# Finishing steps of graph blocks spread over more places of a pipeline, and GpSimd's gathers without a wait in mid group

## What is computed

```
x = gatv2(embed, src, dst, Wl1, ..., heads=4)      # pass 2
x = relu(x)
x = gatv2(x, src, dst, Wl2, ..., heads=1)          # pass 3
# gatv2: xl = x @ Wl + bl ; xr = x @ Wr + br
#   score = (leaky_relu(xl[src] + xr[dst], 0.2) * att).sum()
#   alpha = exp(score - max) / sum over the edges of dst
#   out   = segment_sum(xl[src] * alpha, dst) + bias
# typed layer, twice (its edges: passes 4 and 5):
#   k, q, v = typed_linear(x, ntype, Wk / Wq / Wv)    # one of 8 matrices by node type
#   kw, m   = per head and edge type matrices on k[src], v[src]
#   a = (kw * q[dst]).sum(-1) * pri / sqrt(16);  alpha = segment softmax of a
#   out = silu(typed_linear(segment_sum(alpha * m), ntype, Wa))
#   out = layernorm(out * al + x * (1 - al)) * g + b
```

## Time and profile before

| what | value |
|---|---|
| median of 3 runs | 7276.15 us (7275.86 to 7287.23) |
| profiled execution, its own time | 7268.52 us |
| its span, first to last instruction | 7266.8 us |
| busy share of the span: PE, DVE, ACT, POOL | 68%, 69%, 24%, 66% |
| mean granted clock of TensorE | 0.777 of full |
| HBM traffic over the span | 173 GB/s |

### The profile page before, as it was taken

One profiled execution on the slowest core, in us unless ns is written; L12 is line 12 of the kernel. 1 busy time (PEld: TensorE's weight loads), 2 busy tenths in 40 slices (PEclk: granted clock), 3 DMA queues, 4 the chain that ended last, 5 costly groups with the idle time before them and its releaser, 6 DMA issues. The chain is left out here.

```text
span 7266.8 us, 92453 instructions
## 1 busy us (share of the span) xinstructions
PE 4960.7 (68%) x26319; PEld 4144.5 (57%) x26319; DVE 5007.5 (69%) x14623; ACT 1751.7 (24%) x5241; POOL 4810.0 (66%) x5008
## 2 busy tenths in 40 slices
PE   2555555667775777777687877876777776666666
PEld 2444444666664555665466666655666665566665
DVE  4434434777775888888677777766777775788886
ACT  2334332222222222222122222221222222121111
POOL 3777776777775777776555665537666662777774
PEclk8676766777777888777777887777888887787887
DMA  4544445666664444444344444437666664666665
GB/s 132 169 159 160 159 160 157 212 212 215 212 211 124 152 150 144 144 144 137 122 143 148 147 163 132 144 106 231 222 215 206 222 217 127 217 222 224 222 222 154
DMA packets 408011, 1264.32 MB, mean 174 GB/s; under 512 B 128774, under 2 KB 189958, under 8 KB 321110
## 3 DMA queue, kind: packets, MB, share of 16 engines
q1 hardware_dynamic: 200000, 760.63, 29.1%
q0 software_dynamic: 200240, 492.90, 23.8%
q10 hardware_dynamic: 7270, 4.88, 0.2%
HBM read 1081.15 MB, written 176.88 MB: 173 GB/s over the span
## 5 line engine op out<-in xcount | busy, mean ns | idle before, releaser
L757 POOL DMA_INDIRECT gathered_rows<-table_l,arena x3056 | 2962.8, 969 | 1427.3 <-issue 877.7
L1319 PE MATMUL ps<-weighted_rows,onehot 128*128 128x136 f32 (+2 forms) x8320 | 1616.9, 352 | 903.7 <-DVE acc L1171 899.3
L1319 PEld LDWEIGHTS ps<-weighted_rows,onehot 128*128 128x128 f32 x8320 | 1416.8, 250 | 1076.5 <-DVE weighted_rows L1160 483.5
L1286 PEld LDWEIGHTS ps<-dst_side,onehot_t 128*128 128x128 f32 x8320 | 1310.3, 233 | 403.6 <-issue 318.5
L757 POOL DMA_INDIRECT gathered_rows<-table_l,src_rel_edges x1120 | 1063.6, 950 | 614.5 <-issue 314.7
L1286 PE MATMUL ps<-dst_side,onehot_t 128*128 x8320 | 1390.0, 322 | 98.9 <-DVE products L1079 50.8
L1171 DVE TENSOR_TENSOR acc<-acc,ps 128x136 f32 (+2 forms) x4160 | 1186.8, 285 | 110.0 <-PE ps L1319 28.5
L1093 DVE TENSOR_REDUCE scores<-products 128x16 f32<-128x512 f32 (+2 forms) x1040 | 709.1, 682 | 13.4
L880 PE MATMUL ps<-gathered_rows,onehot 128*128 128x128 f32 x1664 | 335.7, 364 | 487.2 <-ACT gathered_rows L817 483.7
L757 POOL DMA_INDIRECT arena<-table_l,src_rel_edges x544 | 516.4, 949 | 203.4 <-issue 154.5
L1283 PE MATMUL ps<-gathered_rows,ident 128*128 128x512 f32 x832 | 554.1, 753 | 91.7 <-DMA gathered_rows<-table_l,arena 85.9
(11 more groups left out here) (312 smaller groups left out, 6156.0 us busy)
## 6 DMA issues: line engine op xcount, KB each, us to landing
onehot_t<-onehots_turned SPq DMA_DIRECT2D x260, 1024.0 KB
onehot<-onehots SPq DMA_DIRECT2D x260, 1024.0 KB, 5.5
onehots<-onehot SPq DMA_DIRECT2D x52, 1024.0 KB
onehots_turned<-onehot_t SPq DMA_DIRECT2D x52, 1024.0 KB
table_l<-arena SPq DMA_DIRECT2D x50, 1024.0 KB
gathered_rows<-table_l,arena POOLq DMA_INDIRECT x3056, 2.5
segment_flags_sb<-segment_flags SPq DMA_DIRECT2D x1300, 8.2 KB
arena<-type_mask_rows SPq DMA_DIRECT2D x75, 256.0 KB
```

What stands on the lines that cost most here:

```text
L757: pool.indirect_dma_start(out=home(v, t // GC)[:, t % GC, :], out_offset=None, in_=table, in_offset=bass.IndirectOffsetOnAxis(ap=index[:, ...
L1286: ins = nc.tensor.matmul(ps[:, BZ + k, g * P:(g + 1) * P], e.ohT[:, u, t * P:(t + 1) * P], kRows[:, bass.ds(bs[t % 8], D)], start=not gat, ...
L1319: ins = nc.tensor.matmul(ps[:, BP + n % 3, at:at + PW], e.oh[:, u, t, :], exvT[:, t, :], start=True, stop=True)
```

## The change

Three things. GpSimd's extra wait at the third chunk is gone, in all five attention passes. In passes 2 to 5 the steps of a block are given later places: ScalarE's steps stand one or two places behind the TensorE or VectorE step that feeds them, where many shared a place before. The order of the steps of one block stays. The last step (the write) moves from place 22 to 26 in pass 3 and stays in the others.

```
-                if t % GC == 0 and paced:
-                    paced(pool, s, t // GC)
...
-        def paced(pool, s, j):
-            if j == 2 and s >= 2:
-                e.z_ready.wait(pool, a_no, J * (s - 1) + 3)
```

The core of pass 3 and 4 in the code:

```
 class AfterGats ... def pe
-            if d == 4:
+            if d == 8:
                 self.turn(pe, self.e.hN[:, k, :], "h_made", k, "rel_taken", BANDS * k)
-            elif d == 6:
+            elif d == 11:
                 self.key_and_value(pe, k, k + 1)
-            elif d == 7:
+            elif d == 12:
                 self.query(pe)
-            elif 8 <= d < 12:
-                self.relations(pe, k, d - 8)
+            elif d in (14, 16, 18, 20):
+                self.relations(pe, k, (d - 14) // 2)
...
 class AfterTyped ... def act
-            if d == 11:
+            if d == 14:
                 self.take_kv(act, k)
                 self.take_query(act, k)
-            elif 12 <= d < 16:
-                self.take_relations(act, k, d - 12)
+            elif 16 <= d < 20:
+                self.take_relations(act, k, d - 16)
...
 class AfterTyped ... def pe
-            elif d == 10:
+            elif d == 13:
                 self.key_and_value(pe, k, 2 * k + 2)
-            elif d == 11:
                 self.query(pe)
-            elif 12 <= d < 16:
-                self.relations(pe, k, d - 12)
+            elif 15 <= d < 19:
+                self.relations(pe, k, d - 15)
```

More of the change, by code:

```diff
@@ L742, in static, with gather_rows @@
     return isinstance(s, int) and s < below
-def gather_rows(nc, e, block, pass_no, table, index, home, free, free_before, here, buffers, ways, paced=None):
+def gather_rows(nc, e, block, pass_no, table, index, home, free, free_before, here, buffers, ways):
     @block.gpsimd
@@ L938, in attention_pass @@
     with after.S, nc.Block() as block:
-        def paced(pool, s, j):
-            if j == 2 and s >= 2:
-                e.z_ready.wait(pool, a_no, J * (s - 1) + 3)
-        gather_rows(nc, e, block, no, table, index, home, e.exv_ready, 1, here, buffers, ways, paced)
+        gather_rows(nc, e, block, no, table, index, home, e.exv_ready, 1, here, buffers, ways)
         flags_base = [sum(16 * (h + 1) * ((NG + 1 - u) // 2) for h in (4, 4, 1, 8, 8)[0:a_no]) for u in range(2)]
@@ L1936, in dve @@
                 own_shares(self, dve, c, k, 4, self.att).then_inc(S["shares"], 1)
-            elif d == 2:
+            elif d == 3:
                 dve.wait_ge(S["exp_made"], k + 1)
@@ L1946, in act @@
             u = k % 2
-            if d == 1:
+            if d == 2:
                 act.wait_ge(S["shares"], k + 1)
                 nc.scalar.activation(self.scalars(k, 32, 8), self.scalars(k, 32, 8), ACT.Exp).then_inc(S["exp_made"], 1)
-            elif d == 3:
+            elif d == 5:
                 act.wait_ge(S["shares_made"], k + 1)
@@ L1956, in act @@
                 ins.then_inc(S["parts_made"], 1)
-            elif d == 5:
+            elif d == 7:
                 act.wait_ge(S["parts_turned"], k + 1)
@@ L1962, in act @@
                 nc.scalar.activation(e.acc[:, k * AW:(k + 1) * AW], e.acc[:, k * AW:(k + 1) * AW], ACT.Copy, scale=0.0)
-            elif d == 7:
+            elif d == 9:
                 self.take_rows(act, k)
@@ L1970, in pe @@
             u = k % 2
-            if d == 4:
+            if d == 6:
                 pe.wait_ge(S["parts_made"], k + 1)
@@ L1976, in pe @@
                 mm(self.corner, self.by_self[u], e.ident[:, :], start=False, stop=True).then_inc(S["parts_turned"], 1)
-            elif d == 6:
+            elif d == 8:
                 self.project(pe, k)
@@ L2118 @@
 class AfterGats(Typed):
-    LAST = 22
+    LAST = 26
     EARLY = 4
@@ L2149, in sp @@
                 self.load_mask(sp, k, 1)
-            elif d == 22:
+            elif d == 26:
                 self.write(sp, k, self.e.t3_d[0])
@@ L2178, in dve @@
                 self.statistics(dve, c, k, xk, "var")
-            elif d == 3:
+            elif d == 6:
                 self.standard(dve, c, k, "std").then_inc(S["scale"], 1)
-            elif d == 5:
+            elif d == 9:
                 self.by_type(dve, k + 1, k, "q_done", k)
@@ L2197, in act @@
                 nc.scalar.activation(e.acc[:, k * AW:(k + 1) * AW], e.acc[:, k * AW:(k + 1) * AW], ACT.Copy, scale=0.0)
[L2198 removed]
+            elif d == 13:
                 self.take_kv(act, k)
                 self.take_query(act, k)
[L2201 to L2202 removed]
+            elif d in (15, 17, 19, 21):
+                self.take_relations(act, k, (d - 15) // 2)
     def pe(self, pe, x):
         for k, d in self.due(x):
[L2207 removed]
+            if d == 8:
                 self.turn(pe, self.e.hN[:, k, :], "h_made", k, "rel_taken", BANDS * k)
[L2209 removed]
+            elif d == 11:
                 self.key_and_value(pe, k, k + 1)
[L2211 removed]
+            elif d == 12:
                 self.query(pe)
[L2213 to L2214 removed]
+            elif d in (14, 16, 18, 20):
+                self.relations(pe, k, (d - 14) // 2)
 class FromLayer(Typed):
@@ L2261, in layer_dve @@
                 self.statistics(dve, c, k, self.o, "var")
-            elif d == 7:
+            elif d == 10:
                 mean, rstd = self.scalars(k, 24, 1), self.scalars(k, 29, 1)
@@ L2346, in dve @@
         for k, d in self.due(x):
-            if d == 3:
+            if d == 4:
                 self.by_type(dve, 2 * k + 1, k, "q_done", k)
-            elif d == 9:
+            elif d == 12:
                 self.by_type(dve, 2 * k + 2, k, "y_made", k + 1)
@@ L2355, in act @@
         for k, d in self.due(x):
-            if d == 11:
+            if d == 14:
                 self.take_kv(act, k)
                 self.take_query(act, k)
-            elif 12 <= d < 16:
-                self.take_relations(act, k, d - 12)
+            elif 16 <= d < 20:
+                self.take_relations(act, k, d - 16)
     def pe(self, pe, x):
         for k, d in self.due(x):
-            if d == 2:
+            if d == 3:
                 self.turn(pe, self.agg, "agg_made", k, "rel_taken", BANDS * k)
-            elif d == 4:
+            elif d == 5:
                 self.layer_pe(pe, k, 2 * k + 1)
-            elif d == 8:
+            elif d == 11:
                 self.turn(pe, self.e.hN[:, k, :], "h_made", k, "y_taken", k + 1)
-            elif d == 10:
+            elif d == 13:
                 self.key_and_value(pe, k, 2 * k + 2)
-            elif d == 11:
                 self.query(pe)
-            elif 12 <= d < 16:
-                self.relations(pe, k, d - 12)
+            elif 15 <= d < 19:
+                self.relations(pe, k, d - 15)
 class AfterAll(FromLayer):
@@ L2434, in act @@
         for k, d in self.due(x):
-            if d == 9:
+            if d == 12:
                 act.wait_ge(S["turned"], 2 * k + 2)
                 nc.scalar.activation(self.hT, self.corner, ACT.Copy).then_inc(S["h_kept"], 1)
-            elif d == 11:
+            elif d == 14:
                 act.wait_ge(S["last"], k + 1)
```

6 lines of the change are left out of this document (removed).

## The result

Five runs of the changed kernel took 7237.1 us in the median (7226.4 to 7250.5), against 7278.2 for the kernel before on the same chip: a ratio of 0.9943, with a 95% interval of 0.9929 to 0.9957. That is faster by 0.6%, where I had forecast 1.8% (7145). The profiled execution took 7226.4, its span 7224.7, which is 42.1 less than before.

A forecast was written before the change was run, and what follows sets the result against it. GpSimd's floor bounds passes 1 and 5, the VectorE, TensorE, ScalarE ring passes 2 to 4. Savings 94 + 17 + 20 = 131 from 7268.5 give 7137.5; 7.6 for the median makes 7145 us, range 6985 to 7262.

The forecast's parts named there:

- GpSimd's waits, 0: All five attention passes: removing GpSimd's mid-group waits gains 0, as its lead covers them; bound 270.1 us.
- Pass 4, -94: Pass 4: VectorE's 203 us of waits fall to 109 as steps move; 94 us saved, bounds -120 and -25.
- My 4.5 and 4.6: Pass 4: us VectorE still waits per early block (4.5, 13 blocks) and late block (4.6, 11 blocks).
- and 0.4 in the light slot: Pass 4, late blocks: VectorE idles only 0.4 us in the light slot, beside 4.2 in the heavy one.
- Pass 3, -17: Pass 3: early blocks gain 42 us, late ones lose 25; 17 saved in all, bounds -80 and +50.
- 1.8 and 2.6 put product 3 at P + 11.8: Pass 3, late pair's first slot: VectorE's two block steps start product 3 11.8 us after product 0 (P).
- and weighing at P + 15.7: Same slot: weighing starts 15.7 us after product 0, or 2 later at half clock; slot 25.4 us.
- Pass 2, -20: Pass 2: moved projection and part turn save 20 us of VectorE's waits for a product; bounds -35 and +5.
- so I take most: Pass 2: bare slots hardly have the 26.6 us wait before a product, so most of it goes.
- The ends, 0: Ends of the passes: they end in the same chain of steps, so no time is gained or lost.
- B: Rival, passes 3 and 4: TensorE's lumps among destination rows at half clock decide, making it slower; 7315 us, chance 0.11.
- The rule that every lump behind an idle starts slow: Trainium skill's clock rule, pass 3: early pairs take 52.5 us, late ones 54.0; pass 3 +20, sum 94.

The follow-up runs named there:

- waits_alone: The kernel before with GpSimd's wait for destination rows taken out of all five attention passes, no block step moved: 7271.0 us, ratio 1.0002.
- few_relations: Changed kernel with most of TensorE's work for a block's second to fourth relation steps left out (8 columns for 256): 7180.2 us, ratio 0.9879.
- late_hole: Changed kernel with new places for some late-block steps in passes 3 and 4, and own shares' exponential one place earlier in passes 2 and 3: 7109.4 us, 0.9780.
- same_slots: late_hole with early blocks of pass 3 given the late blocks' places in a slot, and pass 2's early scaled shares one place later: 7058.9 us, 0.9707.
- exp_back: Changed kernel with ScalarE's exponential of own shares back at its old place, one earlier, in passes 2 and 3: 7189.1 us, ratio 0.9890.
- by_kind: Changed kernel with all old places for late blocks in passes 2 and 3 and for the last two blocks in passes 4 and 5: 7157.5 us, 0.9848.
- warm_8: same_slots with 8 added TensorE products of 128 columns per slot, results unread, ahead of the third portion of sums: 7146.0 us, ratio 0.9831.

## Why the prediction was wrong, step by step

**GpSimd's waits, 0**: right, shown by waits_alone.

**Pass 4, -94; it was -54.4, 58.0 of it in the window and 3.6 lost at its end.** My 4.5 and 4.6 were what VectorE would still wait for an early and for a late block, 109 us in all. Of the same waits 131.0 are left: by the stretches 42.3 over 13 early blocks, or 3.3 each, and 88.2 over 11 late ones, or 8.0 each. The step that failed is "and 0.4 in the light slot". I had counted what the relation steps and products leave, but not what the relation steps come to stand ahead of: the next block's turned aggregate. VectorE waits 3.4 to 5.0 there, 34.7 in all; few_relations took 24.0 of it away and the pass 26.1, late_hole all but 0.7, for 29.1. The other slot's 4.2 was 4.0. Besides, 72.0 us less of these waits made the window only 58.0 shorter: VectorE's idle time that has no releaser in the profile rose from 25.2 to 61.0, a term that my sum did not have and that stays open.

**Pass 3, -17; it was +3.5: -8.6 in the window and 12.1 at its end.** Early blocks gave 50.0, where I had 42. Their pair was 51.2 us, where I had 51.3, but that is partly luck: its first slot took 27.1 for my 25.0, with a wait of 2.75 for the deviation that I did not have and that same_slots took away, and its second 24.1 for 25.0 to 27.5, as the product took 3.8 us, the time of the full clock. Late blocks lost 43.1, where I had 25. Their pair was 54.6 for 52.0, and the step that failed is "1.8 and 2.6 put product 3 at P + 11.8", and with it "and weighing at P + 15.7": between the 1.8 and the 2.6 VectorE waits 1.5 for the exponential behind the copy, a wait that I had put at nothing, and P + 18.7 came of it. exp_back, where this one step is back, has P + 11.7, P + 15.8 and a pass that is 28.0 shorter. The second slot, which I had given most care, was right (26.8).

**Pass 2, -20; it was +6.5.** Early blocks gained 7.4; late ones lost 17.2 to the same exponential. The step that failed is "so I take most": of the 26.6 before a product 16.0 stayed, and the wait for the exponential, 14.0, came in. Without it the pass is 23.9 shorter, which is -17; that this is close to my -20 is luck, since 16.4 before a product are left in exp_back as well. I had a sum of 131 and the span gave 42: beside the 89 us between them, this one step, forgotten in two passes, is worth 52 by exp_back, and the relation steps of pass 4 some 26 by few_relations. The two runs were made apart, so these need not add.

**The ends, 0**: +22 us by the rows (0.7, 12.1, 3.6 and 5.9 behind passes 2 to 5), of which by_kind shows that in pass 4 they are slots' work that moved behind the last slot, not a loss of its own.

**The rivals.** B was half right: lumps decide in late blocks and take back what others gain, but without making the whole slower. The rule that every lump behind an idle starts slow, by which I had +20 for pass 3, holds for the rows (2.08 behind 3.3 us of idle), but the early pairs came out as without it, and late pairs (54.6, near its 54.0) took 51.3 in exp_back, behind the same slow rows: what they lost was the exponential's. A's 22.0 in pass 3 isn't reached by same_slots either (23.2), its 20.3 in pass 4 nearly (20.9).

## What to carry to other kernels

When a step is moved, ask two things of each engine's queue: what stands ahead of the step at its new place, down to the shortest one (0.20 us of ScalarE cost 52 us over two passes, and 43 of the whole span), and what the step now stands ahead of. Slots that meet the same step at different places need places of their own: one table for two kinds of block gave 0.6%, two tables 2.9%. Long products belong where their engine waits for something else anyway, and that is read from the idle time in its timeline. Work that only fills an idle, as in warm_8, can move the idle, and the slow clock behind it, to rows that are waited for.

## What the hardware showed that I had not expected

The granted clock can be at the lower of its two levels while TensorE is never idle. Three windows inside the pass 4 slot quoted above, changed kernel:

```profile
5395.00:5401.00 6.00, 4.92 (x28) 3.51 (x26) 5.65 (x17) 1.03 (x5) 3.81 (x4) 0.91 0.87 250
5401.00:5411.50 10.50, 10.50 (x35) 8.33 (x35) 5.75 (x19) 4.19 (x17) 7.96 (x9) 0.50 0.65 227
5411.50:5417.40 5.90, 5.90 (x45) 5.85 (x44) 4.70 (x10) 0.40 (x1) 3.39 (x4) 0.82 0.41 114
```

TensorE is busy 10.50 of 10.50 us at 0.50, that is 1.2 GHz, behind an idle of only 1.08 us, while two of the relation steps with 32 rows run and a third ends. In few_relations, where these steps are narrow, the rows behind the drop of such a slot still took 2.05 us, and in late_hole three of the four steps of such a slot take 1.13 us and one 2.07; why the clock is low there stays open. And an added product of 4-byte numbers shows as two entries, so that 24 of them took 5.5 to 7.8 us, twice and more what I had planned from 128-column entries of 0.11.
